# A local attention layer with quarter-array score tiles, one copy of the queries and a row maximum that is negated as it is taken

## What is computed

```
def l2norm(t):
    return t / jnp.maximum(jnp.linalg.norm(t, axis=-1, keepdims=True), 1e-12)
...
q = l2norm(q) * qs
k = l2norm(k) * ksc
q = q * cos * scale + rotate_half(q) * sin * scale
inv = 1.0 / scale
k = k * cos * inv + rotate_half(k) * sin * inv
out = local_attention(q, k, v)
...
sim = jnp.einsum('bhwie,bhwje->bhwij', bq, bk2) * QK_SCALE
sim = jnp.where(mask, -jnp.finfo(sim.dtype).max, sim)
attn = jax.nn.softmax(sim, -1)
```

## Time and profile before

| | |
|---|---|
| time, median of 3 runs | 5210.2 us (5207.42 to 5211.37) |
| the profiled execution: its own time | 5209.42 us |
| the profiled execution: span from first to last instruction | 5207.6 us |
| mean granted clock of TensorE | 0.807 |
| busy share PE, DVE, ACT, POOL | 76%, 72%, 50%, 42% |
| instructions PE, DVE, ACT, POOL | 25476, 7356, 6832, 1600 |
| L948 (once for each unit), in the window 300:2500 | 184, 1224 ns each |

### The profile page before, as it was taken

How to read it: one execution, slowest core, us unless ns; L and a number is a source line. 1 busy time by engine, 2 the same in 40 slices (tenths; PEclk the granted TensorE clock), 3 DMA queues, 4 the chain that set the end, 5 groups by cost and what they waited for, 6 DMA issues and landing times. The chain is left out here.

```text
span 5207.6 us, 75861 instructions
## 1 busy us (share of the span) xinstructions
PE 3957.9 (76%) x25476; PEld 2535.0 (49%) x25476; DVE 3764.7 (72%) x7356; ACT 2578.7 (50%) x6832; POOL 2174.9 (42%) x1600
## 2 busy tenths in 40 slices
PE   5389799799799799799777767956666666587897
PEld 2166466466466466466343343333333333355664
DVE  5799499599599598598363544399999999832343
ACT  2188488488488488488222121233333333335343
POOL 0177277277276376376120310066666666500000
PEclk7699899899899899999777687855555555566998
DMA  0011111111111111111000000000000000000000
GB/s 17 27 42 42 38 42 41 38 43 42 37 40 41 38 41 42 37 42 43 28 1 9 1 25 0 0 1 1 1 1 1 1 1 1 1 7 7 15 1 9
DMA packets 48634, 109.67 MB, mean 21 GB/s; under 512 B 8944, under 2 KB 9200, under 8 KB 46704
## 3 DMA queue, kind: packets, MB, share of 16 engines
q1 hardware_dynamic: 48240, 104.66, 6.6%
HBM read 31.23 MB, written 1.05 MB: 6 GB/s over the span
## 5 line engine op out<-in xcount | busy, mean ns | idle before, releaser
L1084 POOL TENSOR_TENSOR slabs<-slabs 128x512 f32<-128x512 f32 x768 | 976.3, 1301 | 374.5 <-DVE slabs L948 374.5
L1781 DVE MAX8 slabs<-slabs 128x8 f32<-128x512 f32 x1084 | 691.8, 679 | 58.6 <-ACT slabs L1718 58.6
L1807 POOL TENSOR_SCALAR slabs<-slabs 128x512 f32<-128x512 f32 x256 | 400.3, 1564 | 472.6 <-DVE slabs L1787 472.6
L622 PE MATMUL psum<-slabs 128*128 128x512 f32 x768 | 406.4, 655 | 225.8 <-DVE slabs L948 152.1
L1073 POOL TENSOR_TENSOR slabs<-slabs 128x768 f32<-128x768 f32 x192 | 344.1, 1792 | 559.8 <-DVE slabs L925 559.8
L853 ACT ACTIVATE slabs<-slabs 128x96 f32<-128x96 f32 x1536 | 551.5, 360 | 41.8 <-PE psum L666 40.0
L1702 ACT ACTIVATE slabs<-slabs 128x512 f32<-128x512 f32 x316 | 211.6, 719 | 728.3 <-DVE slabs L1787 728.2
L1640 PE MATMUL psum<-constants,slabs 128*128 128x128 f32 x1264 | 304.4, 405 | 302.4 <-POOL slabs L1810 302.1
L1783 DVE MATCH_REPLACE8 slabs<-slabs 128x512 f32<-128x512 f32 x768 | 513.2, 676 | 0.0
L1631 PE MATMUL psum<-slabs 8*128 8x512 f32 (+1 forms) x632 | 348.5, 1092 | 163.9 <-ACT slabs L1718 163.7
L658 PEld LDWEIGHTS psum<-weights,slabs 128*128 128x128 f32 x3072 | 372.2, 192 | 99.9 <-issue 86.1
(11 more groups left out here) (392 smaller groups left out, 8379.1 us busy)
## 6 DMA issues: line engine op xcount, KB each, us to landing
slabs<-slabs SPq DMA_DIRECT2D x192, 192.0 KB, 2.5
slabs<-slabs SPq DMA_DIRECT2D x192, 128.0 KB, 2.5
slabs<-F1A SPq DMA_DIRECT2D x7, 2176.0 KB, 8.4
slabs<-slabs SPq DMA_DIRECT2D x144, 64.0 KB, 2.1
slabs<-F1F SPq DMA_DIRECT2D x6, 580.5 KB, 4.4
slabs<-S SPq DMA_DIRECT2D x4, 645.0 KB, 5.6
weights<-M SPq DMA_DIRECT2D x1, 2184.0 KB, 9.4
weights<-R SPq DMA_DIRECT2D x2, 1079.5 KB, 5.4
```

Source lines behind the costliest of these rows:

```text
L622: last = nc.tensor.matmul(ps[:, i, :], tokens, w(name, 512 * half, 512), start=True, stop=True)
L1084: nc.gpsimd.tensor_tensor(out[:, at, :], normed[:, at, :], table, ALU.mult).then_inc(rope_done, 1)
L1781: nc.vector.max(eight, work[side] if k else scores[slot + side]).then_inc(picked[b], 1)
L1807: nc.gpsimd.tensor_scalar(kept[n % 2], scores[slot], tops[:, slot, TOPK - 1:TOPK], None, ALU.is_ge).then_inc(kept_ready, 1)
```

## The change

- `score` issues 16 products where it issued 8, each on a quarter of the array: 64 rows (one head of a pair) and 64 columns (one window of queries), 96 keys.
- The queries are then needed without zeros: `qT` replaces `qBD`, one copy of all 128 rows replaces two of 64 rows, and the clearing of `qBD` at the start goes.
- The clamp L937 goes from DVE. ACT computes a Relu and a logarithm with an offset in place of the one logarithm, and the first refining instruction takes the maximum itself.
- The factor 8 stands in the table of the queries' cosines and sines, and the maximum is negated by the instruction that takes it, so L977 and its semaphore go.
- The mask of the first tile is one tensor, so that `mask_scores` is one addition there too.
- Scores, probabilities and their transposes are kept in another order of heads and windows. The order of the stages on each engine is as it was.

```diff
             def score(u):
...
-                for n in range(GROUPED):
-                    c, k = n // 2, n % 2
-                    keys = kT[:, PAIRS * half + c, t * P + k * WINDOW:t * P + k * WINDOW + KEYS]
-                    last = nc.tensor.matmul(SCORES[:, n // 4, n % 4, :], qBD[:, c, k, :, :], keys, start=True, stop=True)
+                for n in range(GROUPED):
+                    c, h = n // 2, n % 2
+                    for k in range(2):
+                        keys = kT[64 * h:64 * h + 64, PAIRS * half + c, t * P + k * WINDOW:t * P + k * WINDOW + KEYS]
+                        queries = qT[64 * h:64 * h + 64, c, k * WINDOW:k * WINDOW + WINDOW]
+                        last = nc.tensor.matmul(ps[k * WINDOW:k * WINDOW + WINDOW, 4 + h, KEYS * c:KEYS * c + KEYS], queries, keys,
+                                                start=True, stop=True)
...
             def root_of_sum(u):
-                act.wait_ge(root_step, ROOT_STEPS * u + 2)
-                nc.scalar.activation(logs, sums, ACT.Ln, scale=LIFT).then_inc(logged, 1)
-                act.wait_ge(logged, u + 1)
+                act.wait_ge(root_step, ROOT_STEPS * u + 1)
+                nc.scalar.activation(logs, sums, ACT.Relu, scale=LIFT, bias=m.tiny[:, 2:3]).then_inc(logged, 1)
+                act.wait_ge(logged, 2 * u + 1)
+                nc.scalar.activation(logs, logs, ACT.Ln, bias=m.tiny[:, 3:4]).then_inc(logged, 1)
+                act.wait_ge(logged, 2 * u + 2)
                 nc.scalar.activation(root, logs, ACT.Exp, scale=-0.5).then_inc(rooted, 1)
...
-                for h in range(2):
-                    rows = slice(64 * h, 64 * h + 64)
-                    nc.scalar.activation(qBD[rows, :, :, h, :], QT[rows, :, :, :], ACT.Copy).then_inc(qT_copied, 1)
+                nc.scalar.activation(qT, QT, ACT.Copy).then_inc(qT_copied, 1)
...
             def sum_squares(u):
-                step = Chain(dve, root_step, ROOT_STEPS * u)
                 dve.wait_ge(squared, u + 1)
-                step(nc.vector.tensor_reduce(sums, squares, axis=AX.X, op=ALU.add))
-                nc.vector.tensor_scalar(sums, sums, 1e-24, None, ALU.max).then_inc(root_step, 1)
+                nc.vector.tensor_reduce(sums, squares, axis=AX.X, op=ALU.add).then_inc(root_step, 1)
...
-                step(nc.vector.tensor_tensor(grown, root, sums, ALU.mult))
+                step(nc.vector.scalar_tensor_tensor(out=grown, in0=sums, scalar=LEAST, in1=root, op0=ALU.max, op1=ALU.mult))
...
-                nc.vector.tensor_reduce(tops, masked, axis=AX.X, op=ALU.max).then_inc(masked_step, 1)
-                dve.wait_ge(masked_step, MAX_STEPS * u + 2)
-                nc.vector.tensor_scalar(shifts, tops, -8.0, None, ALU.mult).then_inc(shift_ready, 1)
+                nc.vector.tensor_reduce(shifts, masked, axis=AX.X, op=ALU.max, negate=True).then_inc(masked_step, 1)
```

More of the change, by code:

```diff
@@ L476 @@
 UNITS = 2 * (TOK // P)
+LIFT, LEAST = 2.0 ** 20, 1e-24
+QK_SCALE = 8.0
 GROUPED = 2 * PAIRS
@@ L522, in _ @@
             nc.gpsimd.memset(shifted[:, :, 0:REACH], 0.0)
-            nc.gpsimd.memset(m.slab(7)[:, 256:1280], 0.0)
             nc.gpsimd.memset(m.slab(16, 2), 0.0)
     with nc.Fori(0, F1_LAYERS) as layer:
-        local_layer(nc, m, ins, layer, w, for_attention, for_forward, angles, tables, shifted, qBD, hA, hB)
+        local_layer(nc, m, ins, layer, w, for_attention, for_forward, angles, tables, shifted, qT, hA, hB)
     with phase(nc, "silu_done") as (block, silu_done):
@@ L532, in _, with local_layer @@
             nc.scalar.activation(g_out.rearrange("p (b t) -> p b t", b=BATCH), hA[:, :, 1:PADSEQ], ACT.Silu)
-def local_layer(nc, m, ins, layer, w, for_attention, for_forward, angles, tables, shifted, qBD, hA, hB):
+def local_layer(nc, m, ins, layer, w, for_attention, for_forward, angles, tables, shifted, qT, hA, hB):
     ps = m.psum
@@ L549, in local_layer @@
     logs, grown, root = (small[:, 16 + 16 * i:32 + 16 * i] for i in range(3))
-    tops, denom, inverse, shifts = (small[:, 80 + 8 * i:88 + 8 * i] for i in range(4))
+    denom, inverse, shifts = (small[:, 80 + 8 * i:88 + 8 * i] for i in range(3))
     v = [m.slab(16 + n // 2)[0:KEYS, 1024 * (n % 2):1024 * (n % 2) + 1024].rearrange("p (k d) -> p k d", k=2) for n in range(4)]
@@ L573, in local_layer @@
     MIX, OWN = 6, 7
-    ROOT_STEPS, MAX_STEPS = 5, 2
-    LIFT = 2.0 ** 20
+    ROOT_STEPS, MAX_STEPS = 4, 2
     def place(u):
@@ L678, in weigh @@
                         last = nc.tensor.matmul(ps[rows, 3, WINDOW * n:WINDOW * n + WINDOW], v[u % 4][:, k, c * P + 64 * h:c * P + 64 * h + 64],
-                                                turned[0:KEYS, c, k, rows], start=True, stop=True)
+                                                turned[0:KEYS, PAIRS * h + c, k * WINDOW:k * WINDOW + WINDOW], start=True, stop=True)
                 last.then_inc(pv_product, 1)
@@ L845, in copy_probs @@
                     act.wait_ge(pv_product, u)
-                nc.scalar.activation(turned[0:KEYS, 2 * part:2 * part + 2, :, :], PT, ACT.Copy).then_inc(pT_copied, 1)
+                nc.scalar.activation(turned[0:KEYS, 4 * part:4 * part + 4, :], PT, ACT.Copy).then_inc(pT_copied, 1)
             def exponential(u):
-                act.wait_ge(shift_ready, u + 1)
+                act.wait_ge(masked_step, MAX_STEPS * u + 2)
                 if u >= 1:
@@ L852, in exponential @@
                 for n in range(GROUPED):
-                    last = nc.scalar.activation(probs[:, n, :], masked[:, n, :], ACT.Exp, bias=shifts[:, n:n + 1], scale=8.0,
+                    last = nc.scalar.activation(probs[:, n, :], masked[:, n, :], ACT.Exp, bias=shifts[:, n:n + 1],
                                                 accum_out=denom[:, n:n + 1])
@@ L963, in mask_scores @@
                     dve.wait_ge(exp_done, u)
[L964 to L972, removed]
+                shape = mask[1 if t else 0].rearrange("p (o r j) -> p o r j", o=1, r=1).broadcast_to([P, 2, 4, KEYS])
+                last = nc.vector.tensor_tensor(masked.rearrange("p (b n) j -> p b n j", b=2), SCORES, shape, ALU.add)
                 last.then_inc(masked_step, 1)
                 dve.wait_ge(masked_step, MAX_STEPS * u + 1)
-                nc.vector.tensor_reduce(tops, masked, axis=AX.X, op=ALU.max).then_inc(masked_step, 1)
-                dve.wait_ge(masked_step, MAX_STEPS * u + 2)
-                nc.vector.tensor_scalar(shifts, tops, -8.0, None, ALU.mult).then_inc(shift_ready, 1)
+                nc.vector.tensor_reduce(shifts, masked, axis=AX.X, op=ALU.max, negate=True).then_inc(masked_step, 1)
             step = Chain(dve, own)
@@ L2456, in constants @@
     tiny[:, 1] = 1e-6
+    tiny[:, 2], tiny[:, 3] = -LIFT * LEAST, LIFT * LEAST
     return pack(CONST_PARTS, {
@@ L2474, in rotary_tables @@
     cos, sin = np.cos(freqs), np.sin(freqs) * sign
-    kinds = np.stack([a.astype(f) for a in (cos * scale, sin * scale, cos * inv, sin * inv)], 1)
+    kinds = np.stack([a.astype(f) for a in (QK_SCALE * cos * scale, QK_SCALE * sin * scale, cos * inv, sin * inv)], 1)
     return f(1024) * kinds.reshape(4, P, 4, HD1).transpose(1, 0, 2, 3).reshape(P, -1)
@@ L2483, in window_masks @@
     seen = (q <= k) & (k <= q + REACH)
-    return np.concatenate([np.where(s, 0, MASKED) for s in (seen & (k >= REACH), seen)], 1).astype(np.float32)
+    first = np.arange(P)[:, None] >= WINDOW
+    return np.concatenate([np.where(s, 0, MASKED) for s in (seen & ((k >= REACH) | first), seen)], 1).astype(np.float32)
 def pad_cols(a, n):
```

18 lines of the change are left out of this document (9 added, 9 removed).

## The result

The changed kernel takes 5309.7 us (5302.8 to 5318.3), the kernel before beside it 5210.1 us (5207.4 to 5211.4). The ratio is 1.0196, with 95% bounds of 1.0183 and 1.0208: 99.5 us slower, where 18 us less were forecast.

What follows compares the result with a forecast made beforehand. It took POOL's four products and the last wait for them, not busy DVE, to bound the step. Terms 2.2 + 0.85 + 0.5 - 0.1 - 0.5 = 3.0 us a layer, 18 in six, gave 5191 us, range 5168 to 5208.

Steps and rivals of the forecast that it cites:

- the one on the score product: Score on PE, 1.92 to 1.4 us: covered in the middle of a layer, gain 0.5 us at its end.
- Rival 4: PE's clock granted at half for longer: one more such project a layer gives 5203, two 5215; chance 0.10, half slower.
- The terms for the small edits: Clamp, L977 and refining edits on DVE and ACT: 2.2 + 0.85 - 0.1 - 0.5 = 2.45 us gain a layer.
- rival 1: POOL's queued product goes before the waiting DVE instruction: 2.2 us a layer lost, 5205 us; chance 0.15.
- 15 steps of that kind: Steps 4, 5, 6 and even ones 8 to 30, without L931: clamp's removal gains 0.15 us each, 2.2 a layer.
- 0.85: Exponentials on ACT no longer behind the clamp's wait, so L925 after step 3 starts 0.85 us sooner, once a layer.
- the 0.4 of the refining instruction: First refining instruction on DVE takes 0.175 us instead of 0.16, always on the path: 0.5 us lost a layer.
- Rival 2: DVE really is the bound: both removed instructions' whole time returns, 350 us, giving 4859; chance 0.05 for this large form.
- Rival 3: Quarter tiles don't overlap: a score takes 3.85 us on PE, 218 us slower, 5430; chance 0.05.
- the lower bound of 1.15: Score's 32 passes on PE following each other like L678's, 0.036 us each: 1.15 us.
- The layer's end: Last score runs straight into L700 and PE sets the time: gain 0.5 us a layer, bounds +0.8 and -1.9.
- The range's lower end, 5168: Fastest time in the forecast's range, where the odd steps gain and the layer's end does too.

Runs made afterwards that it cites:

- small edits alone: Kernel before with clamp moved to ACT and the refining step, negated maximum, factor 8 in the tables, score unchanged: 5202.6 us, ratio 0.9995.
- the split: Changed kernel with one 128x128 product put into the middle of PE's idle stretch in even steps, waiting for DVE: 5278.8 us, ratio 1.0139.

## Why the prediction was wrong

**The step that failed** is the one on the score product: "In the middle of a layer this is covered: an even step leaves PE idle 1.10 us before the next project". A longer score can indeed use up that idle time. A shorter one adds to it, and the sum put this at 0. It costs the clock: 2.13 us of idle time instead of 1.10, then a project of 3.66 us instead of 1.98, on the path that sets the step.

**Rival 4** named the clock, and "PE's clock below 1.00 inside a layer" as its sign. Its reason, "less of the array at work", is not what the runs show: twice the quarter tiles keep the clock, and half the scores on the full array lose it. Its size was wrong by nearly ten too: one or two projects a layer, where 65 of 72 pairs are hit, eleven a layer. The 65 times 1.65 us are 107 us. The undisturbed gains of the middle take 10 off it, and 98 are what the windows show. The mistake lay in reading 1.00 as a state that lasts. The row did not tell how near the edge it stood: between one and a half scores and two, a third of a microsecond of work in an even step decides whether a layer pays 12 us (245.5 for 233.0).

**The terms for the small edits** hold in their sum. L957 takes 1.74 us (about 1.8 forecast), L943 1.24 (1.2), POOL's handed-over product 1.72 (1.7), so rival 1 falls. In the middle of a layer the kernel with these edits alone gains 1.6 us. Twelve of the 15 steps of that kind lie there, 1.8 us, and less the 0.4 of the refining instruction 1.4 was forecast. In the first six steps it gains 0.8, where 0.85 + 0.45 - 0.2 = 1.1 was forecast. In the changed kernel L928 of step 4 still has [0.44] before it, where almost none was expected (DVE in time):

```profile
656.98 1.22 DVE L949 TENSOR_TENSOR slabs<-psum,slabs 128x1024 f32<-128x1024 f32 x1
658.65 0.20 DVE L928 RECIPROCAL slabs<-slabs 128x8 f32<-128x8 f32 x1 [0.44 <-ACT slabs L856]
```

That is 0.57 less than the 1.01 of the earlier trace rows, where 0.85 was taken. One price was off, and it is part of that shortfall: ACT's instructions with an offset from a tensor take 0.31 us, not 0.216, so that L943 waits in the steps 0 to 2. ACT in time there:

```profile
638.87 0.31 ACT L813 ACTIVATE slabs<-slabs,constants 128x16 f32<-128x16 f32 x1 [1.29 <-DVE slabs L938]
639.21 0.31 ACT L815 ACTIVATE slabs<-slabs,constants 128x16 f32<-128x16 f32 x1
639.54 0.21 ACT L817 ACTIVATE slabs<-slabs 128x16 f32<-128x16 f32 x1
```

**Rival 2** falls: in the kernel with the small edits alone, at full clock, DVE's busy time is 35 us less in 25 steps (189.29 for 224.28), and the steps are 1.7 us shorter. **Rival 3** falls on the other side: a score takes 0.89 us, below even the lower bound of 1.15, where 1.4 was taken. The prediction worked out from which length on a slow score loses, and never asked from which length on a quick one does.

**The layer's end.** From step 31 to the next layer's step 0 it is 93.4 to 95.8 us before and 93.7 to 95.8 after. The 0.5 us of gain forecast there can't be seen; 15 to 33 us of half clock fall into this part in the several kernels, and that moves it by more. The range's lower end, 5168, follows from no sum shown: the odd steps give 5179, and the best layer's end 0.3 x 6 = 2 us more.

**If the clock is kept**, about two thirds of the 18 us come. From the end of `normalise` in step 0 of the first layer to that in step 31 of the sixth it is 2202.3 us before, 2190.6 with the small edits alone and 2190.0 with the score issued twice: 12 us. Against their own runs of before, the score issued twice gains 11.6 us, twice in even steps 10.2, queries turned twice 8.2, the values twice 7.9. These are the versions that beat the kernel before too, by 0.1 to 0.3%.

**Left open.** What quantity the clock goes by isn't settled: the longest stretch is ruled out, the sum of idle time orders the kernels but for the split. Why some pairs escape in a kernel where most are hit isn't either. And the small edits alone gain 14 us in the profiled execution and nothing that can be told in the medians. What comes behind step 31 of the sixth layer is nearly all code that the change leaves alone, and it takes 2759 to 2774 us in the twelve profiled executions; such a spread can hide the gain, but only one execution of each kernel is in a trace.

## What to carry to other kernels

Where TensorE idles a little in every round and its clock is still full, a shorter product there may not be free: work out how much idle time a round would have behind the change, and price a round at half clock before the change is called covered. The remedy can be work that is thrown away, put into the round that lacks it (0.66 us in each second step took back the 100 us here). A granted clock of 1.00 tells that it holds, and nothing of how far it is from falling: it was 1.00 with 1.51 us of idle time in a pair (before) and with 2.22 (score twice in even steps). A cheap test is to take some work away from the kernel before (half the scores here) and read the clock.

## What was not expected of the hardware

- The clock falls and returns inside a steady loop: 3.4 us at 1.2 GHz, 17.1 us at 2.4, in nearly every pair of steps, with PE busy 86% of the time (215.04 / 251.34) and no idle stretch above 2.2 us. The busy share of the 25 steps doesn't tell the cases apart: it is 88% with the score twice in even steps (205.84 / 232.96), where no pair is hit, and 88% with the split (213.93 / 243.76), where 47 are. A share taken at half clock counts the slow project as busy.
- Quarter-array passes of 64 rows and 64 columns streaming 96 columns follow each other at 0.028 us (0.89 / 32), at 0.024 in a row of 64 (1.55 / 64), where one full-array pass of the same product took 0.120: four of them in less time than one of the other. Row L630 behind L660 begins with no gap (843.70, where L660 ends at 843.77; the ends are modelled), so a change of tile size cost nothing that can be seen. The Trainium skill, "TensorE: Matmul & The Clock Gate", section "LDWEIGHTS", gives a load's time as columns / 1.2 ns, 53 ns for 64. The passes here are faster than that would allow if the loads came one at a time.
- When a DVE instruction waits for the third POOL product and a fourth is queued, DVE goes first. This holds in all 72 even steps of the middle (L957 1.74 to 1.75 us, POOL's fourth 1.71 to 1.73 in place of 1.26).
